# Two state-space scans on one core: in every second state of layer 1 GpSimd forms two of the three products with C, rows start 8 bytes further, and ScalarE's side work is spaced differently

## The reference, cut to what matters

```python
# layer 1: B,C per position and state n (16 of them), delta per position and channel (192)
def step(hc, inp):
    u_t, d_t, B_t, C_t = inp
    hc = hc * jnp.exp(d_t[..., None] * A[None]) + (d_t * u_t)[..., None] * B_t[:, :, None, :]
    return (hc, jnp.einsum('bkdn,bkn->bkd', hc, C_t))
...
# layer 3
dA = dlt[..., None] * A_log[None, :, :, None, :]
phi = jnp.exp(-jnp.cumsum(dA, axis=3))
dbx = dlt[..., None] * jnp.swapaxes(b, 2, 3)[:, :, None] * xs[..., None]
h = phi * jnp.cumsum(dbx / (phi + 1e-12), axis=3)
y = jnp.einsum('bkdln,bknl->bkdl', h, c) + Ds[None, :, :, None]
```

## Time and profile before

| | us |
|---|---|
| median of 3 runs | 16709.1 (16696.06 to 16725.33) |
| the profiled execution, its own time | 16707.54 |
| its span, first to last instruction | 16705.6 |
| DVE busy | 14926.7 |
| POOL busy | 12620.4 |
| ACT busy | 12298.3 |
| PE busy | 13571.3 |

### The profile page before, as it was taken

How to read it: one execution, slowest core, us unless ns; L and a number is a source line. 1 busy time by engine, 2 the same in 40 slices (tenths; PEclk the granted TensorE clock), 3 DMA queues, 4 the chain that set the end, 5 groups by cost and what they waited for, 6 DMA issues and landing times. The chain is left out here.

```text
span 16705.6 us, 189354 instructions
## 1 busy us (share of the span) xinstructions
PE 13571.3 (81%) x38048; PEld 5620.9 (34%) x38048; DVE 14926.7 (89%) x20527; ACT 12298.3 (74%) x27189; POOL 12620.4 (76%) x6313
## 2 busy tenths in 40 slices
PE   7988978888888878888888886877777777777777
PEld 2222223333333333333333333533333333333333
DVE  6666669999999988999999996889999988999998
ACT  3555567777777766777777774588888968888996
POOL 0000059999999978999999994289999968999996
PEclk9999989999999999999999998988888888888988
DMA  1100023333333333333333332122222212222221
GB/s 24 19 14 17 5 74 113 112 113 112 111 111 111 111 96 107 112 113 113 111 111 111 111 111 80 49 78 85 85 84 83 84 48 80 85 85 84 83 84 46
DMA packets 543207, 1404.94 MB, mean 84 GB/s; under 512 B 135566, under 2 KB 191926, under 8 KB 539430
## 3 DMA queue, kind: packets, MB, share of 16 engines
q1 hardware_dynamic: 542034, 1392.84, 29.0%
HBM read 1311.24 MB, written 58.30 MB: 82 GB/s over the span
## 5 line engine op out<-in xcount | busy, mean ns | idle before, releaser
L1415 POOL TENSOR_TENSOR Tr<-du,BC 128x1344 f32<-128x1344 f32 x2688 | 8174.7, 3041 | 138.5 <-DVE du L1283 137.2
L1079 PE MATMUL PS<-Hc,ident 128*128 128x448 f32 x16128 | 7115.6, 578 | 1363.7 <-POOL Hc L1424 1133.9
L1079 PEld LDWEIGHTS PS<-Hc,ident 128*128 128x128 f32 x16128 | 3063.8, 199 | 5308.9 <-issue 2706.6
L1200 ACT ACTIVATE PS<-dl,A 128x448 f32<-128x448 f32 x5376 | 3401.9, 633 | 1599.8 <-DVE Hr L1333 1054.9
L1424 POOL TENSOR_TENSOR Hc<-Hr,BC 128x448 f32<-128x448 f32 (+1 forms) x2688 | 3603.9, 1341 | 602.2 <-DVE Hr L1333 527.1
L1333 DVE TENSOR_TENSOR_SCAN PS<-PS,Tr 128x449 f32<-128x449 f32 x3584 | 3711.0, 1078 | 93.0 <-ACT st L1216 82.4
L1340 DVE TENSOR_TENSOR Hc<-PS,BC 128x448 f32<-128x448 f32 x4480 | 2568.9, 607 | 0.0
L1210 ACT ACTIVATE PS<-cs,lneps,A 128x448 f32<-128x448 f32 x2688 | 1935.1, 720 | 18.8 <-DVE PS L1333 1.0
L1333 DVE TENSOR_TENSOR_SCAN Hr<-PS,Tr 128x449 f32<-128x449 f32 x1792 | 1938.4, 1082 | 0.0
L1333 DVE TENSOR_TENSOR_SCAN Hr<-Ar,PS 128x449 f32<-128x449 f32 x1792 | 1931.7, 1078 | 0.0
L1315 DVE SCALAR_TENSOR_TENSOR PS<-PS,Tr 128x448 f32<-128x448 f32 x2688 | 1651.1, 614 | 223.2 <-ACT PS L1210 203.6
(11 more groups left out here) (271 smaller groups left out, 15394.8 us busy)
## 6 DMA issues: line engine op xcount, KB each, us to landing
BC<-bcscratch SPq DMA_DIRECT2D x5376, 224.0 KB, 3.6
zscratch<-zst SPq DMA_DIRECT2D x84, 224.0 KB, 1.9
bcscratch<-rows SPq DMA_DIRECT2D x336, 56.0 KB, 1.7
z<-zscratch SPq DMA_DIRECT2D x28, 672.0 KB, 4.8
xg<-mid SPq DMA_DIRECT2D x12, 1176.0 KB, 7.9
xr<-mid SPq DMA_DIRECT2D x56, 168.0 KB, 2.7
rl<-rows SPq DMA_DIRECT2D x56, 168.0 KB, 3.3
Q<-part SPq DMA_DIRECT2D x72, 98.0 KB, 4.4
```

Of the source, the lines that this page charges most:

```text
L1079: e.matmul(PS[:, YB + c, 0:T], K["ident"][:], Hc[:, g % NHC, c, :], start=False, stop=(nn == 15)).then_inc(y_done, 1)
L1200: e.activation(decay_at(u, 1), dl[:, q % 2, c, :], ACT.Exp, scale=A[:, q // NT, c, nn:nn + 1]).then_inc(a_done, 1)
L1415: e.tensor_tensor(Tr[:, g % NTR] if ratio else Tr[:, g % NTR, :, 1:TW], du[:, q % 2], b, ALU.mult).then_inc(t_done, 1)
```

## The change

(1) In layer 1 `on_dve(g)` is 2 in even and 1 in odd states: in odd states the scan of c = 1 goes to Hr and its product to POOL, whose instruction is then 2x448. `products_before` counts DVE's products. (2) Rows of dl, du and Hr are padded to 452 elements and start so that what POOL reads begins at byte 8 of each 16 in a row; all of Tr stays where it was. (3) In layer 1 `keep_psum` stands ahead of the merge and side step in its slot. (4) The last `delta` of layer 1 is a slot earlier. In layer 3 the side steps are further apart and later, and three logarithms become one instruction. (5) PE's `total` sums dl and du first and the logarithm last.

```diff
-    ON_DVE = 1 if ratio else 2
+    def on_dve(g):
+        return 1 if ratio else 2 - g % 2
+    def products_before(g):
+        return g if ratio else g + (g + 1) // 2
...
-    TW = T + 1
+    TW, TP = T + 1, T + 4
...
-        xs, dl, du = sb("xs", [128, 3, T]), sb("dl", [128, 2, 3, T]), sb("du", [128, 2, 3, T])
+        xs = sb("xs", [128, 3, T])
+        dl, du = (sb(i, [128, 2, 3, TP])[:, :, :, 2:2 + T] for i in ("dl", "du"))
...
-        Hr = sb("Hr", [128, NH, 3 - ON_DVE, TW])
+        Hr = sb("Hr", [128, NH, 2, TP])[:, :, :, 1:1 + TW]
...
-            return PS[:, HB + c, first:TW] if c < ON_DVE else Hr[:, g % NH, c - ON_DVE, first:TW]
+            return PS[:, HB + c, first:TW] if c < on_dve(g) else Hr[:, g % NH, c - 1, first:TW]
...
             def total(q, c):
-                e.wait_ge(minus, q + 1 if ratio else 3 * q + c + 1)
-                e.matmul(X_, K["ident"][:], du[:, s, c, :], start=True, stop=False)
+                e.wait_ge(expd, 3 * q + c + 1)
+                e.matmul(X_, K["ident"][:], dl[:, s, c, :], start=True, stop=False)
+                e.matmul(X_, K["ident"][:], du[:, s, c, :], start=False, stop=False)
+                e.wait_ge(minus, q + 1 if ratio else 3 * q + c + 1)
                 e.matmul(X_, K["nident" if ratio else "ident"][:], w1[:, c, :], start=False, stop=False)
                 e.wait_ge(logd, 3 * q + c + 1)
-                e.matmul(X_, K["ident"][:], logs(q)[:, c, :], start=False, stop=False)
-                e.matmul(X_, K["ident"][:], dl[:, s, c, :], start=False, stop=True).then_inc(x_full, 1)
+                e.matmul(X_, K["ident"][:], logs(q)[:, c, :], start=False, stop=True).then_inc(x_full, 1)
...
             def logs_together(q, i):
-                for c in range(3):
-                    loga(q, c)
+                e.wait_ge(expd, 3 * q + 3)
+                if q:
+                    e.wait_ge(cs_ready, 3 * q)
+                e.activation(logs(q)[:], du[:, q % 2], ACT.Ln, bias=K["one"][:]).then_inc(logd, 3)
...
-                SIDE = {gather: (5, 7, 8), rows_or_dts: (10, 11), absolute: (13, 17, 21), positive: (14, 18, 22),
-                        expo: (16, 20, 23), logs_together: (25,), delta: (32, 36, 41)}
+                SIDE = {gather: (5, 7, 10), rows_or_dts: (13, 14), absolute: (16, 20, 25), positive: (17, 22, 26),
+                        expo: (19, 23, 28), logs_together: (29,), delta: (34, 38, 42)}
...
-                        delta: (29, 35, 41)}
+                        delta: (29, 35, 40)}
...
+                if c == 1 and not ratio:
+                    keep_psum(g)
                 if q and s in MERGE:
...
-                if c == 1:
+                if c == 1 and ratio:
                     keep_psum(g)
...
-            AFTER = (33, 37, 42) if ratio else (31, 37, 42)
+            AFTER = (35, 39, 43) if ratio else (31, 37, 42)
...
-                e.tensor_tensor(Hc[:, g % NHC, ON_DVE:3], Hr[:, g % NH, :, 1:TW], c_, ALU.mult).then_inc(hp_done, 1)
+                e.tensor_tensor(Hc[:, g % NHC, m:3], Hr[:, g % NH, m - 1:2, 1:TW], c_, ALU.mult).then_inc(hp_done, 1)
```

More of the change, by code:

```diff
@@ L1039, in total @@
                 e.wait_ge(x_free, use(q, "total", c) if q else use(q, "delta", c) + 1)
-                e.wait_ge(minus, q + 1 if ratio else 3 * q + c + 1)
                 if c and q:
                     e.wait_ge(total_read, 3 * q + c)
-                e.matmul(X_, K["ident"][:], du[:, s, c, :], start=True, stop=False)
+                e.wait_ge(expd, 3 * q + c + 1)
+                e.matmul(X_, K["ident"][:], dl[:, s, c, :], start=True, stop=False)
+                e.matmul(X_, K["ident"][:], du[:, s, c, :], start=False, stop=False)
+                e.wait_ge(minus, q + 1 if ratio else 3 * q + c + 1)
                 e.matmul(X_, K["nident" if ratio else "ident"][:], w1[:, c, :], start=False, stop=False)
                 e.wait_ge(logd, 3 * q + c + 1)
-                e.matmul(X_, K["ident"][:], logs(q)[:, c, :], start=False, stop=False)
-                e.matmul(X_, K["ident"][:], dl[:, s, c, :], start=False, stop=True).then_inc(x_full, 1)
+                e.matmul(X_, K["ident"][:], logs(q)[:, c, :], start=False, stop=True).then_inc(x_full, 1)
             def prepare(q, r):
-                if r == 3:
+                first = 4 if ratio else 3
+                if r == first:
                     proj(q)
-                elif r in (4, 5):
-                    pre_delta(q, r - 4)
+                elif r in (first + 1, first + 2):
+                    pre_delta(q, r - first - 1)
                 elif r == 6 and not ratio:
                     pre_delta(q, 2)
-                elif r == (10 if ratio else 9):
+                elif r == 9 and not ratio:
                     total(q, 0)
-                elif r == 11 and ratio:
-                    total(q, 1)
             def prepare_late(q, r):
-                if r == 6 and ratio:
+                if ratio and r == 7:
                     pre_delta(q, 2)
[L1064 to L1067, removed]
+                elif ratio and 10 <= r < 13:
+                    total(q, r - 10)
+                elif not ratio and r in (10, 12):
+                    total(q, r // 2 - 4)
             def gather_n(g):
@@ L1074, in gather_n @@
                         seed(q, c)
-                    if c < ON_DVE:
-                        e.wait_ge(h_done, ON_DVE * g + c + 1)
-                    elif c == ON_DVE:
+                    if c < on_dve(g):
+                        e.wait_ge(h_done, products_before(g) + c + 1)
+                    elif c == on_dve(g):
                         e.wait_ge(hp_done, g + 1)
@@ L1155, in loga @@
                 e.wait_ge(expd, 3 * q + c + 1)
-                if ratio and q:
-                    e.wait_ge(cs_ready, 3 * q)
                 e.activation(logs(q)[:, c, :], du[:, q % 2, c, :], ACT.Ln, bias=K["one"][:]).then_inc(logd, 1)
@@ L1213, in keep_psum @@
             def keep_psum(g):
-                nn = g % 16
-                e.wait_ge(h_done, ON_DVE * (g + 1))
-                e.activation(st[:, nn, 0:ON_DVE], PS[:, HB:HB + ON_DVE, T], ACT.Copy).then_inc(st_done, 1)
+                nn, m = g % 16, on_dve(g)
+                e.wait_ge(h_done, products_before(g + 1))
+                e.activation(st[:, nn, 0:m], PS[:, HB:HB + m, T], ACT.Copy).then_inc(st_done, 1)
             def keep_sbuf(g):
-                nn = g % 16
+                nn, m = g % 16, on_dve(g)
                 e.wait_ge(s_done, 3 * g + 3)
-                e.activation(st[:, nn, ON_DVE:3], Hr[:, g % NH, :, T], ACT.Copy).then_inc(st_done, 1)
+                e.activation(st[:, nn, m:3], Hr[:, g % NH, m - 1:2, T], ACT.Copy).then_inc(st_done, 1)
             def seed(g):
@@ L1244, in act @@
                 positive(0, c)
-            for step in (expo, loga) if ratio else (expo, one_plus, minus_w, loga):
+            for step in (expo,) if ratio else (expo, one_plus, minus_w, loga):
                 for c in range(3):
                     step(0, c)
+            if ratio:
+                logs_together(0, 0)
             for c in range(3):
@@ L1302, in prepare @@
             def prepare(q, s):
-                if ratio and s == 26:
+                if ratio and s == 30:
                     one_less(q)
@@ L1326, in scan @@
                     e.wait_ge(t_done, g + 1)
-                if c < ON_DVE and g:
-                    e.wait_ge(h_done, ON_DVE * (g - 1) + c + 1)
+                if c < on_dve(g) and g:
+                    e.wait_ge(h_done, products_before(g))
                     e.wait_ge(st_done, 2 * g - 1)
-                elif c >= ON_DVE and g >= NH:
+                elif c >= on_dve(g) and g >= NH:
                     e.wait_ge(hp_done, g - NH + 1)
@@ L1376, in dve @@
                     prepare(q + 1, 3 * r + 1)
-                for c in range(ON_DVE):
+                for c in range(on_dve(g)):
                     project(g, c)
@@ L1421, in project @@
                     e.wait_ge(y_done, 3 * (g - NHC) + 3)
-                m = 3 - ON_DVE
-                c_ = BC[:, g % NBS, 1:2, :].broadcast_to([128, m, T])
-                e.tensor_tensor(Hc[:, g % NHC, ON_DVE:3], Hr[:, g % NH, :, 1:TW], c_, ALU.mult).then_inc(hp_done, 1)
+                m = on_dve(g)
+                c_ = BC[:, g % NBS, 1:2, :].broadcast_to([128, 3 - m, T])
+                e.tensor_tensor(Hc[:, g % NHC, m:3], Hr[:, g % NH, m - 1:2, 1:TW], c_, ALU.mult).then_inc(hp_done, 1)
             e.memset(yacc[:], 0.0).then_inc(y_init, 1)
@@ L1462, in spread @@
                     e.wait_ge(t_done, g - NBS + 1)
-                    e.wait_ge(h_done, ON_DVE * (g - NBS + 1))
+                    e.wait_ge(h_done, products_before(g - NBS + 1))
                     e.wait_ge(hp_done, g - NBS + 1)
```

## The result

The changed kernel takes 16074.8 us, median of four runs (16054.84 to 16078.17), against 16712.8 for the kernel before beside it: ratio 0.9616, 95% interval 0.9600 to 0.9633. That is 638 us less, where 593 were forecast; 16115 was predicted, 16000 to 16400 the range.

The account below looks back on a forecast made before the run. DVE was taken as layer 1's bound, POOL 3.6 us a tile behind, and DVE as layer 3's. Gains of 531 us (layer 1) and 62 (layer 3), 593 off 16707.5, gave 16115; range 16000 to 16400.

Parts of the forecast that it names:

- The two sums of layer 1: Layer 1, instruction costs summed per tile: DVE falls from 65.9 to 61.8 us, POOL from 63.7 to 61.9.
- the input price at which the change breaks even: POOL in layer 1: the kernel gets slower if an input instruction costs more than 2.88 us.
- the 62 us of layer 3: Layer 3: DVE's waits for ACT's weight shrink, 1.1 us a tile over 56 tiles.
- The st and delta waits: Layer 1: DVE's waits for st (0.82 us a tile) and for the last delta (0.33) should go.
- the early copy: Layer 1, `keep_psum` ahead of the side step: DVE's scan no longer waits for st, 0.82 us a tile.
- first rival: Layer 1: ACT becomes the pace, adding 1.6 us a tile while today's 1.44 of waits stay; 16365 us, chance 0.18.
- The remainder: Layer 1: 0.3 us a tile unexplained plus 0.4 for POOL and DVE interfering, giving 62.6.
- nothing is late there: Layer 1, ACT's side step after DVE's product: 0.56 us fits in one Hr scan (1.00) before the next decay.
- the sign that the prediction had set for its first rival: Layer 1: DVE idle before scans, released by ACT's decay; that rival's chance was 0.18.
- 531: Layer 1: gain in us from a tile falling from 67.34 to 62.6 us, over 112 tiles.
- DVE's instructions are the same: Layer 3: DVE's tile stays at the sum of its instructions; only waits can change.
- the third rival: Wide POOL products cost more beside DVE, 2.45 us against 1.93, making POOL's tile 66.1; 16511 us, chance 0.04.

Follow-up runs that it names:

- rows_only: The kernel before with only dl, du and Hr starting at byte 8; 16712.7 us, ratio 1.0001.
- split_only: The kernel before with only the new division of products between VectorE and GpSimd, rows and side work as before; 17121.9 us, ratio 1.0241.
- du_at_4: The kernel after with the rows of dl and du at byte 4 instead of 8; 16839.2 us in a single run.
- bc_at_8: The kernel after with the rows of B and C at byte 8 as well; 17328.5 us in a single run.
- side_only: The kernel before with the new side work, early st copy, order of total and joined logarithm, products and rows as before; 16502.3 us, ratio 0.9873.
- split_rows: The kernel before with the new division of products and the rows at byte 8, side work as before; 16485.2 us, ratio 0.9862.
- late_keep: The kernel after with layer 1's copy of st behind the merge and side step again; 16349.7 us, ratio 0.9782.
- du_0_bc_8: The kernel after with dl and du back at byte 0, B and C at byte 8, Hr still at byte 8; 16437.7 us in a single run.

## Why the prediction was right

**The two sums of layer 1.** VectorE 61.8 and GpSimd 61.9 us a tile were forecast, and the tile is 62.3. They come from starts in the timeline, not from durations or busy time. Sums made in this way held in the other runs too: rows_only leaves VectorE's 65.9 plus waits standing, and where GpSimd is the bound its tile came out at 70.8 us for 71 (split_only), 69.1 for 69.2 (du_at_4) and 73.0 for 73 (bc_at_8). One side remark of the sum was off: the input price at which the change breaks even, 2.88 us, leaves out the 62 us of layer 3. With them it is (67.3 + 0.55 - 21.2) / 16 = 2.92, so about a sixth of the saving would have been enough, not a quarter.

**The waits.** The st and delta waits went as forecast, and with the old rows and products that was worth 144 us in layer 1 (side_only), where the two waits were 129. The forecast's sum needed only that the wait for st be gone. What the prediction did not see is how much hung on it: it priced the early copy at today's wait, 0.82 us a tile, and left behind merge and side step the wait would have grown to 2.43 (split_rows), so that late_keep loses 275 us, 2.46 us a tile. The prediction's first rival, that ACT becomes the pace, gave 16365, and late_keep took 16349.7. That the times are close is chance: of the 3.0 us a tile that the rival added 1.6 were late decays, and in late_keep VectorE waits for st and never for a decay. The growth sits behind the states with one product (73.1 of 100.6 us), and there VectorE's scans into the bank follow each other after 3.49 us (from 3502.20 to 3505.69 in the kernel after) where they took 4.02, so ScalarE has that much less time for the same list.

**The remainder.** 0.7 us a tile was added: 0.3 that the sum of today had left unexplained, and 0.4 for VectorE and GpSimd in each other's way. Measured is 0.53, and it is a wait for a decay once a tile. So the size was near by luck, for another reason than the one given. It also contradicts the prediction's step that with the early copy "nothing is late there", and it is the sign that the prediction had set for its first rival, at a third of the 1.6 us that this rival put on it. The unexplained 0.3 has a likely source: two scans last 2.06 us and the next instruction starts after 1.97, so each wait costs its idle time and some 0.09 us of lost overlap. The kernel before had 140 such waits in 43 tiles, which makes 0.29 us a tile, an estimate; split_rows, with 271 in 41.4 tiles, has 0.5 beyond its sum and its waits. Layer 1 gave 568 us for 531, 37 of the 45 by which the forecast was short.

**Layer 3.** 62 us forecast, 69 measured. VectorE's wait for the weight was 91.8 us in 23.6 tiles, 3.9 a tile; after the change it is 50.7 in 21.6, 2.3 a tile. Of that 2.1 is the change of tables, and the rest fell from 1.2 to 0.3, as forecast. But "DVE's instructions are the same" did not hold: `one_less` became dearer, which the wait behind it hides. Two rows of VectorE's timeline in layer 3 of the kernel after:

```profile
10741.06 1.54 DVE L1300 TENSOR_SCALAR w<-du 128x1344 f32<-128x1344 f32 x1
10744.67 0.63 DVE L1325 SCALAR_TENSOR_TENSOR PS<-PS,Tr 128x448 f32<-128x448 f32 x1 [2.07 <-ACT PS L1216]
```

It took 0.83 us before, and the wait behind it was 2.68; now 1.54 and 2.07. From its start to the next instruction it is 3.5 us before and 3.6 after, because ScalarE's change of tables sets the end. These changes account for 0.8 of the 1.2 us by which a tile fell; the rest is not traced.

The cheap `one_less` had a price on the other engine. In the kernel before, the GpSimd product that starts beside it takes 2.45 us and not 1.93, in the first two rows here; in side_only, where a product is already running when it starts, it takes 1.29 itself and GpSimd's next input 3.65 instead of 3.04 (last three rows):

```profile
11035.33 0.83 DVE L1290 TENSOR_SCALAR w<-du 128x1344 f32<-128x1344 f32 x1
11035.49 2.45 POOL L1424 TENSOR_TENSOR Hc<-Hr,BC 128x896 f32<-128x896 f32 x1 [0.41 <-DVE Hr L1333]
...
10992.42 1.92 POOL L1428 TENSOR_TENSOR Hc<-Hr,BC 128x896 f32<-128x896 f32 x1
10993.77 1.29 DVE L1294 TENSOR_SCALAR w<-du 128x1344 f32<-128x1344 f32 x1
10994.30 3.65 POOL L1419 TENSOR_TENSOR Tr<-du,BC 128x1344 f32<-128x1344 f32 x1
```

This is what the third rival had seen in its 2.45. After the change no product of GpSimd takes more than 1.80 us and `one_less` takes 1.54 every time, so with the gap between the rows neither holds up the other.

## What to carry to other kernels

Before moving work between two engines, sum both lists for one period from starts in the timeline: here each half of the change alone was worth nothing or less, and together they win (233 us even with the old side work), because the move needs the room that the cheaper rows make. A wait of today's profile is no price for an order that protects the engine once the period is shorter; ask what each small copy stands behind, and take it back alone to see. And on GpSimd, look at the addresses of the two inputs of a dear instruction: a start at another byte of 16 was worth a sixth of its time here.

## What the runs showed of the hardware

- GpSimd's fp32 product of two SBUF inputs costs 0.95 us for each row of 448 when the first input starts 0 or 4 bytes (modulo 16) after the second, and 0.79 us when 8 or 12 (12 by the products of the kernel before alone), with 0.19 us a time on top: 3.04 and 2.57 us for three rows, 2.09 and 1.77 for two, 1.13 and 0.98 for one. Where the output starts made no difference (Tr had starts at 0, 4, 8 and 12 before).
- VectorE's `tensor_scalar` on 1344 elements from SBUF takes 0.83 us when its input is one run and GpSimd is idle as it starts (before). It takes 1.53 to 1.54 when the input is three rows of 448 in a pitch of 452, at byte 0 (du_0_bc_8: 1.538), 4 (du_at_4: 1.539) and 8 (after: 1.540). In rows_only, with the side work still in its old place, it is 1.527. So it is the gap between the rows, not the start and not the new place; whether their number matters was not tested.
- In the one-run form it and GpSimd's two-input products hold each other up: 0.52 us more for a product (before), or 0.46 more for itself and 0.6 more for GpSimd's next input (side_only). With the gap neither is held up.
- GpSimd's durations can overlap the next instruction's: in du_at_4 an input reads 3.38 us at 3004 us and 3.21 at 5000 us where the next instruction starts 2.99 us later, and 3.04 in layer 3 of the same run. Its rate did not change, so starts can be summed there and durations cannot. What stretches them is open: in bc_at_8 GpSimd waits as little in layer 1, and its inputs read 3.03 to 3.04.
